# Second products of the layers and experts as three float16 products

## What is computed

```python
def experts(xf, ...):                       # layer 0: 1 shared layer of 256, layer 1: 2 of 256; 8 experts of 128
    shared = silu(xf @ w1) * (xf @ w3) @ w2
    s = sigmoid(concat([xf, tf]) @ router_W)
    gates = top 2 of 8 by s + bias, normalised
    routed = sum_e gates[:, e] * (gelu(xf @ W1e[e]) @ W2e[e])
    return (shared + routed) / n
x = x + experts_0(x); x = x + experts_1(x)
def step(h, z_t):                           # 256 steps, one after the other
    gate = sigmoid(h @ Wh.T + z_t @ Wz.T + b)
    return tanh(h * (1 - alpha) + gate * z_t)
x = x + scan(step, cond, x); x = x + attention(x, image, mask)   # 16 heads of 8
```

## Time and profile before

| | us |
|---|---|
| median of 3 runs (lowest, highest) | 564.74 (562.11, 565.25) |
| the profiled execution | 564.28 |
| its span | 562.5 |
| busy: TensorE, VectorE | 485.3, 430.2 |
| busy: ScalarE, GpSimd | 251.5, 124.7 |
| first tanh of the recurrence, last one | 47.5, 400.7 |

### The profile page before, as it was taken

The page is one execution under the profiler, slowest core; times in us unless marked ns, Lnnn a source line. Parts: engine busy times, 40 slices in busy tenths (PEclk is TensorE's granted clock), DMA queues, the critical chain, the costliest instruction groups (busy, mean ns, idle before and its releaser), DMA issues.

```text
span 562.5 us, 12896 instructions
## 1 busy us (share of the span) xinstructions
PE 485.3 (86%) x4166; PEld 306.4 (54%) x4166; DVE 430.2 (76%) x1747; ACT 251.5 (45%) x1038; POOL 124.7 (22%) x202
## 2 busy tenths in 40 slices
PE   4899998898999989999988778687698699998993
PEld 2577675665766757667653345243353365545440
DVE  5677888987888878887876999888638877666643
ACT  3332534445455454544547534443338534334460
POOL 5220131541011111001000051523302052222320
PEclk9899998998999989999999869887779899999998
DMA  8300000000000000000000000000000000000000
GB/s 310 154 1 1 2 2 2 2 2 1 2 2 1 2 2 1 2 2 1 2 1 1 2 1 2 1 1 2 1 20 1 7 14 1 2 1 20 3 0 20
DMA packets 4914, 8.39 MB, mean 15 GB/s; under 512 B 496, under 2 KB 3824, under 8 KB 4720
## 3 DMA queue, kind: packets, MB, share of 16 engines
q1 hardware_dynamic: 4416, 7.29, 3.7%
q10 hardware_dynamic: 432, 0.27, 0.2%
HBM read 6.51 MB, written 1.05 MB: 13 GB/s over the span
## 4 chain that ended last, share of the span: by engine, by line
PE 69%; DVE 14%; ACT 8%; issue 5%; POOL 2%; DMA 1%; ACTq 0%; DVEq 0%; POOLq 0%
PE ybk L820 13%; PE hid L943 12%; PE ybk L923 6%; PE cbk L965 5%; PE cbk L962 4%; DVE vbk L1253 3%; PE hid L901 3%; PE cbk L923 3%; PE hid L908 3%; PE hid L806 2%; DVE hlo L1240 2%; DVE d L1242 2%; PE hid L875 2%; ACT hhi L744 2%; PE hid L878 2%
## 5 line engine op out<-in xcount | busy, mean ns | idle before, releaser
L943 PE MATMUL hid<-xsp,up 128*128 128x256 f16 x672 | 101.4, 295 | 1.6 <-DVE up L1022 1.4
L634 POOL TENSOR_TENSOR lm<-cz,mneg 128x512 bf16<-128x512 bf16 x64 | 64.8, 1043 | 161.1 <-DVE mneg L1175 88.5
L732 ACT ACTIVATE d<-cbk 128x8 f32<-128x8 f32 x256 | 45.7, 179 | 117.0 <-PE cbk L966 115.6
L820 PE MATMUL ybk<-hg,down 128*128 128x256 f32 x352 | 97.2, 399 | 0.9 <-DVE hg L1123 0.8
L962 PEld LDWEIGHTS cbk<-hhi,wh 128*128 128x128 bf16 x768 | 44.8, 99 | 74.6 <-ACT hhi L744 64.0
L1253 DVE TENSOR_TENSOR_SCAN vbk<-d 128x16 f32<-128x16 f32 x256 | 56.7, 222 | 30.7 <-ACT d L732 26.3
L744 ACT ACTIVATE hhi<-vbk 128x8 f16<-128x8 f32 x255 | 45.0, 177 | 76.3 <-DVE vbk L1253 76.3
L962 PE MATMUL cbk<-hhi,wh 128*128 128x8 f16 x768 | 58.6, 170 | 21.3 <-ACT hhi L744 19.2
L722 ACT ACTIVATE hb<-hid,att 128x512 f32<-128x512 f32 x78 | 51.9, 688 | 42.4 <-PE hid L908 42.4
L943 PEld LDWEIGHTS hid<-xsp,up 128*128 128x128 f16 x672 | 62.8, 103 | 14.0 <-issue 1.9
L1166 DVE TENSOR_REDUCE wm<-hid 128x2 f32<-128x256 f32 (+2 forms) x105 | 56.6, 548 | 14.2 <-PE hid L878 14.1
(11 more groups left out here) (176 smaller groups left out, 807.4 us busy)
## 6 DMA issues: line engine op xcount, KB each, us to landing
qz<-up_in SPq DMA_DIRECT2D x3, 512.0 KB, 7.7
kp<-maskr_in SPq DMA_DIRECT2D x1, 1024.0 KB, 12.0
out_dram<-silu SPq DMA_DIRECT2D x4, 256.0 KB, 2.4
x<-x_in SPq DMA_DIRECT2D x7, 128.0 KB, 8.7
att<-att_in SPq DMA_DIRECT2D x1, 817.0 KB, 10.1
down<-down_in SPq DMA_DIRECT2D x1, 768.0 KB, 9.4
down<-down_in SPq DMA_DIRECT2D x1, 640.0 KB, 6.9
qz<-up_in SPq DMA_DIRECT2D x1, 256.0 KB, 4.7
```

What stands on the lines that cost most here:

```text
L634: i = nc.gpsimd.tensor_tensor(lm[:, b % 2, J * g:J * g + J, :], cz[:].rearrange("p (o k) -> p o k", o=1).broadcast_to([P, J, QT]), mneg[:, ...
L820: m = pe.matmul(ybk[l][:, 0:n], D(l, "w2" if shared else "e2", e * f + i), hg[:, hg_of[made] % NHG, i * n:i * n + n], start=first and i == ...
L943: m = pe.matmul(into, up[:, pw, a:a + P], x_part(c, l, px, slice(0, n)), start=j == 0, stop=j == 2)
```

## The change

The second products become three float16 products as well. The weights "down" are loaded into the landing space "raw" beside the others and split into two float16 parts (unit WD: a copy times 256 on ScalarE, the remainder on VectorE), once per layer. For each unit Y there is a new unit H: ScalarE copies "hg" (512 columns) to float16, GpSimd subtracts that from "hg" for the remainder, both into "hp", which has four buffers. Y then waits for GpSimd and issues six matmuls of 256 columns with float16 operands in place of two with float32. "hg" is now released by H's subtraction, "hp" by Y. The scale of the gates goes from 256 to 16. "nimg" of the attention moves into the space of "hp".

The core of the diff:

```diff
-LATE = ("E", "S", "K", "Q")
+LATE = ("E", "S", "K", "Q", "H")
-GS = 256.0
+GS = 16.0
+DS = 256.0
+NHP = 4
+DOWN_OF = (0, DOWN["w2", 1][0]), (DOWN["w2", 1][0], N_DOWN)
...
+            add(("WD", l), 0, 200 + n * .9, 60 + n * 1.05, False, (("W", l, i), "dve", "act"))
...
-                add(("Y", c, l, "s", i), fs * mm4(n), 0, 0, False, (("SB", c, l, i), "dve", "pe"),
+                add(("H", c, l, "s", i), 0, 600, 0, False, (("SB", c, l, i), "dve", "act"))
+                add(("Y", c, l, "s", i), fs * mm3(n), 0, 0, False, (("H", c, l, "s", i), "pool", "pe"),
...
-                add(("Y", c, l, "e", i), f * mm4(n), 0, 0, False, (("M", c, l, i), "dve", "pe"),
+                add(("H", c, l, "e", i), 0, 600, 0, False, (("M", c, l, i), "dve", "act"))
+                add(("Y", c, l, "e", i), f * mm3(n), 0, 0, False, (("H", c, l, "e", i), "pool", "pe"),
...
+    pool += [(slot_of[k] + 1, *k) for k in hp_users]
...
-        down = sb("down", [P, N_DOWN])
+        down = sb("down", [P, 2, N_DOWN], F16)
+        hp = sb("hp", [P, NHP, 2, 512], F16)
...
+                elif kind == "H":                     # GpSimd
+                    pool.wait_ge(act_done, nth["act", key])
+                    tts(hp[:, i % NHP, 1, 0:n], hg[:, i % NHG, 0:n], hp[:, i % NHP, 0, 0:n], ALU.subtract).then_inc(lo_made, 1)
...
+                elif kind == "WD":                    # ScalarE
+                    act.wait_ge(in_down[l], 16)
+                    nc.scalar.activation(down[:, 0, a:b], raw_down[:, a:b], ACT.Copy, scale=DS).then_inc(act_done, 1)
+                elif kind == "H":
+                    act.wait_ge(dve_done, nth["dve", ("M" if of == "e" else "SB", c, l, e)])
+                    if i >= NHP:
+                        act.wait_ge(pe_done, nth["pe", ("Y",) + hp_key[i - NHP][1:]])
+                    nc.scalar.activation(hp[:, i % NHP, 0, 0:n], hg[:, i % NHG, 0:n], ACT.Copy).then_inc(act_done, 1)
...
-                    pe.wait_ge(dve_done, nth["dve", made])
+                    pe.wait_ge(lo_made, nth["pool", made])
...
-                        m = pe.matmul(ybk[l][:, 0:n], D(l, "w2" if shared else "e2", e * f + i),
-                                      hg[:, hg_of[made] % NHG, i * n:i * n + n], start=first and i == 0,
-                                      stop=last_y[c, l] == key and i == f - 1)
+                        for j, (pw, ph) in enumerate(((0, 0), (0, 1), (1, 0))):
+                            m = pe.matmul(ybk[l][:, 0:n], D(pw, l, "w2" if shared else "e2", e * f + i),
+                                          hp[:, hp_of[made] % NHP, ph, i * n:i * n + n],
+                                          start=first and i == 0 and j == 0,
+                                          stop=last_y[c, l] == key and i == f - 1 and j == 2)
...
+                elif kind == "WD":                    # VectorE
+                    i = stt(down[:, 1, a:b], raw_down[:, a:b], DS, down[:, 0, a:b], ALU.mult, ALU.subtract)
```

More of the change, by code:

```diff
@@ L97, in plan @@
             *([(("RC", 0, 0), "dve", "act")] if l else []))
+        if l != (PIECES[i + 1][0] if i + 1 < len(PIECES) else None):
+            n = DOWN_OF[l][1] - DOWN_OF[l][0]
+            add(("WD", l), 0, 200 + n * .9, 60 + n * 1.05, False, (("W", l, i), "dve", "act"))
     for c in range(NC):
@@ L258, in plan @@
                 ok = end in step_slot and step_slot[end] + 2 <= s
-            if ok and ("C", 0) not in slot_of and key[0] not in ("W", "WH", "XS", "C"):
+            if ok and ("C", 0) not in slot_of and key[0] not in ("W", "WD", "WH", "XS", "C"):
                 ok = key[1] <= 1 and ("W", 0, 0) in slot_of
@@ L267, in plan @@
                 k = hg_users[-NHG]
-                y = ("Y", k[1], k[2], "e", k[3]) if k[0] == "M" else ("Y", k[1], k[2], "s", k[3])
-                ok = y in slot_of and slot_of[y] + 1 <= s + lat["dve"]
+                split = ("H", k[1], k[2], "e" if k[0] == "M" else "s", k[3])
+                ok = split in slot_of and slot_of[split] + 4 <= s + lat["dve"]
+            if ok and key[0] == "H":
+                ok = hg_users[len(hp_users)] == (("M" if key[3] == "e" else "SB"), key[1], key[2], key[4])
+                if ok and len(hp_users) >= NHP:
+                    k = ("Y",) + hp_users[-NHP][1:]
+                    ok = k in slot_of and slot_of[k] + 1 <= s + 1
             if ok and key[0] in ("M", "SB") and key[1]:
@@ L338, in plan @@
     parts["pool"] = [u[1:] for u in sorted(pool)]
-    for key in parts["pool"]:
-        if key[0] == "RG":
-            nth["pool", key] = sum(k[0] == "pool" for k in nth) + 1
-    return parts, nth, steps, bank_of, before, hg_of, hb_of, n_slots
+    for kind in ("RG", "H"):
+        for i, key in enumerate(k for k in parts["pool"] if k[0] == kind):
+            nth["pool", key] = i + 1
+    hp_of = {k: i for i, k in enumerate(hp_users)}
+    return parts, nth, steps, bank_of, before, hg_of, hb_of, hp_of, n_slots
 def x_users(c, l):
@@ L359, in build @@
 def build(nc, x_in, small_in, up_in, down_in, rec_in, att_in, maskr_in, out):
-    parts, nth, steps, bank_of, before, hg_of, hb_of, n_slots = plan()
+    parts, nth, steps, bank_of, before, hg_of, hb_of, hp_of, n_slots = plan()
     with ExitStack() as ctx:
@@ L489, in S, with D @@
             return small[:, a:a + n]
-        def D(l, name, i):
+        def D(part, l, name, i):
             a, _ = DOWN[name, l]
-            return down[:, a + i * P:a + i * P + P]
+            return down[:, part, a + i * P:a + i * P + P]
+        raw_down = raw[:, N_UP:N_UP + N_DOWN]
         def x_part(c, l, part, cols):
@@ L513, in build @@
         hb_key = sorted(hb_of, key=hb_of.get)
+        hp_key = sorted(hp_of, key=hp_of.get)
         kq_key, s_key, sa_key = order_of(("KP", "QP"), "act"), order_of(("S",), "act"), order_of(("SA",), "act")
@@ L810, in unit @@
                     shared = of == "s"
-                    made = ("SB" if shared else "M", c, l, e)
-                    pe.wait_ge(dve_done, nth["dve", made])
+                    made = ("H", c, l, of, e)
+                    pe.wait_ge(lo_made, nth["pool", made])
                     first = first_y[c, l] == key
```

36 lines of the change are left out of this document (26 added, 10 removed).

## The result

The changed kernel takes 634.25 us, median of four runs (633.2 to 635.71), against 563.42 us for the kernel before, median of four runs on the same chip (559.98 to 565.25): a ratio of 1.128, 95% interval 1.124 to 1.132. The forecast was 628 us.

A forecast was written before the change was run, and what follows sets the result against it. A three-engine chain of 1.19 us a step, not TensorE, bounds the recurrence. 562.5 + 60.5 (blocked steps) - 7 (TensorE, small excesses) + 8 (before the steps) + 2 (attention), plus 1.8 around the span, gave 628 us; range 600 to 655.

The forecast's parts named there:

- The lock: In a recurrence step, the scan on VectorE waits until GpSimd's SBUF-reading operation is over; 0.41 us read from one step.
- The sum: Whole kernel: 562.5 + 60.5 - 7 + 8 + 2 = 626.0 us of span, 1.8 us around it, said as 628.
- Length and place of the subtraction: GpSimd's 512-column subtraction takes 1.15 us, starts 0.06 us into the next step, ahead of the scan; 101 us in all.
- Rival (d): GpSimd slower than the slope says: subtraction 1.34 us, adding 14 us, 642 us; chance 0.22 together with rival (b).
- The price: Recurrence steps behind a copy: 0.84 us more for each subtraction, a step of 2.03; 72 of them, 60.5 us.
- Rival (a): Cheaper blocking in the steps: GpSimd's operations run back to back at 0.60 us each, 43 us, total 610 us; chance 0.20.
- The term of −7: Taken off: 4 us for TensorE's shorter products, 3 us for small step excesses that a longer step hides.
- the prelude: Before the first step: weight splits, late copy and subtraction, ten subtractions ahead of the halving of x; +8 us (+3 to +13).
- rival (b): TensorE's clock falls more often, so unblocked steps take at least 1.44 us: 15 us, 643; chance 0.22 together with Rival (d).
- Attention: After the last step: two of 48 attention-value units move there at about 1 us each, +2 us.

The follow-up runs named there:

- the run with 16 columns: The changed kernel with GpSimd's subtraction covering only the first 16 of 512 columns, other low parts zero: 563.18 us, ratio 0.999 to the kernel before.
- the cast: The changed kernel with a GpSimd cast of 512 float32 zeros in place of the subtraction: 583.15 us, ratio 1.034 to the kernel before.
- the write: The changed kernel with GpSimd only writing 1300 columns of an unused tile in place of the subtraction: 575.70 us, ratio 1.021 to the kernel before.
- the pieces: The changed kernel with each GpSimd subtraction cut into four of 128 columns, nothing left out: 604.14 us, ratio 1.074 to the kernel before.
- four products without the lock: The changed kernel with a subtraction of 16 columns and a fourth float16 product in each unit: 567.18 us, ratio 1.009 to the kernel before.

## Why the prediction held, step by step

- **The lock: right.** That a GpSimd instruction that reads SBUF holds a VectorE instruction with two SBUF inputs until it ends was read from one step with a subtraction of 0.67 us and one block of L634. The conclusion was right, but one size was not: the scan of the earlier trace rows was not due at 157.31, since VectorE had two operations of the router in front of it (the timeline of the kernel before, VectorE alone):

```profile
157.33 0.24 DVE L1073 MAX8 mx<-sl 128x8 f32<-128x8 f32 x2
157.48 0.43 DVE L1253 TENSOR_TENSOR_SCAN vbk<-d 128x16 f32<-128x16 f32 x1
```

  So of the 0.41 us by which L744 came late, only some 0.2 were the lock (0.43 us of scan for 0.20). The sum was not hurt, because it went by the end of L558 plus 0.08 us. The same rows show that L1073, with one SBUF input, is not held: the two lie inside L558 at their usual 0.16 us each. The page of the Trainium skill cited there says the same ("SBUF — State Buffer", "Who interferes with whom"), with the exemption for a GpSimd instruction that only writes. The runs agree with all three parts: a cast of 0.62 us holds the scan, a write of 1.18 us does not, and L1199 and L1175 with one input in PSUM are not held.
- **Length and place of the subtraction: right.** 1.15 us forecast, 1.156 measured; 101 us of GpSimd forecast, 101.2 measured; start at 0.06 us of the step forecast, 0.09 measured. Rival (d), at 1.34, is out.
- **The price: right for a lone copy, slightly high in the sum.** 0.84 us and a step of 2.03 were forecast, 0.89 and 2.08 measured after a lone copy, by 0.03 us of later start and the rest behind the scan. But the subtractions whose slot also holds an E start earlier and cost 0.52, so that by the run with 16 columns the 72 cost 57.4 us (0.80 each) in place of 60.5. Rival (a), 0.60 each, is out, for the reason given: each subtraction waits for its own copy.
- **The term of −7: wrong, the largest miss.** I credited 4 us for shorter products and 3 for small excesses that a longer step would hide. All that is not the price came to +9.8 us in the steps instead. Where it lies can be read from the run with 16 columns, as far as two single executions allow.
  - The 4 us were not there: without any long operation the 192 steps of the new plan take 252.8 us, the same as before (252.6). The shorter products help in this plan (a fourth product adds 3.6 us there, 6 us in all), but the slots with a copy and an E last 1.57 us on the mean, those with an E alone 1.36. The prediction had put these twelve slots at nothing; they are some 2.5 us.
  - 2.2 us are the first step (3.67 us for 1.48), which I had counted in the prelude, and 1.2 lie in the 64 steps beside attention.
  - 6.2 us lie in the 119 steps that follow no copy; I had put those at 1.19 us, and they last 1.39 on the mean (1.34 with 16 columns). In 29 of them TensorE's products run at the lower clock, in 5 with 16 columns, and the 29 hold all of the excess. A unit of six then takes 1.44 us instead of 0.81:

```profile
337.05 1.44 PE L868 MATMUL ybk<-hp,down 128*128 128x256 f16 x6
```

  This is rival (b), at under half of its 15 us. The granted clock of the stretch is 0.87 against 0.96 (0.83 to 0.90 in the four traces with the full lock, 0.93 to 0.97 in the five with a shorter lock or none), and TensorE's second products took 89.5 us in the change where the 97.2 of before should have shrunk by a quarter, as they did with 16 columns (72.8). In the four traces with the full lock the steps without a copy last 1.39 to 1.41 us on the mean, in those with 16 columns, the cast, the write, the pieces and four products without the lock 1.34 to 1.39. Why the clock falls more often under the lock, no run isolates.
- **The prelude: the sum right, its parts wrong.** 8 us forecast; 7.5 to the first tanh and 2.5 more in the first step. I had put 3.5 on the weight splits on VectorE and 4 on the row of subtractions. The run with full subtractions only behind the first step shows 7 to 8 us for GpSimd's part, and the one with 16 columns, weight splits and all, is no slower than before. Executions differ here by several us (first tanh at 46.3 and 53.4 in two kernels with the same GpSimd work), so that the rest can't be settled.
- **Attention: wrong sign.** +2 us forecast for two units moved behind the last step; the span from the last tanh to the end fell by 3.4 us. In all nine traces with this plan it lies between 156.8 and 158.6 us, whatever GpSimd does in the steps, against 161.8 before and 159.7 in the kernel before with float16 products. So it comes with the new order; what in the order does it is open. The count of units was a poor measure.
- **The sum.** 53.5 + 8 + 2 forecast, 67.2 + 7.5 − 3.4 measured, on 562.5. The 634 lies only 6 us above 628 in part by luck: the steps outside the price missed by 17 us, and the price (−3), attention (−5) and the prelude (−0.5) gave back half of it. The 192 steps alone, forecast at 305 us, took 319.

## What to carry to other kernels

Before work goes to GpSimd because it is idle, look for VectorE instructions with two SBUF inputs on the path. Here each GpSimd instruction that reads SBUF held them until it ended, so its price in a step was its length less about 0.27 us, roughly the time from its start to the usual end of the scan, whatever the table of busy shares said. Moving it elsewhere in the step moved the lock with it; cutting it into four brought the price from 0.89 to 0.35 us a step, and an instruction that only writes was free in the step. No run that keeps the full split of the values came back to the time of the kernel before; the two that came out below it left the values, or their low halves, out. A gain on an engine that does not end the waits (here 26 us of TensorE, 8 of them real) should not be entered into the sum once another term makes that engine wait longer.

## What the runs showed of the hardware that I had not expected

- Operations of 0.217, 0.616 and 1.156 us beside the same scan make steps of 1.19, 1.53 and 2.08 us after a lone copy. The two long ones cost their length less about 0.27 us; the short one was free.
- Four back-to-back GpSimd instructions do not keep VectorE out: a waiting one gets in behind each piece, and more work in smaller pieces (137.7 us for 101.2) was 30 us faster.
- A subtraction of 512 columns with float16 output takes VectorE 0.703 us and GpSimd 1.156, a ratio of 1.6.
- Under the lock TensorE's granted clock in the 192 steps was 0.87 (0.97 with 16 columns), and its second products took 89.5 us in place of 72.8. The run that only writes lost 12 us without any lock, with a late first step and a granted clock of 0.93; what of it is the clock's is not shown.
